# A gather of 128 rows by index, taken from GpSimd and fetched row by row by SyncE and ScalarE

## The chip, the cores and the metric

The kernel runs on one core of a Trainium2 chip. The metric is the device time of one execution in microseconds (us). GpSimd (POOL in the profile), VectorE (DVE), ScalarE (ACT), TensorE (PE) and SyncE (SP) each run their own instruction stream. SP and ACT can also start plain DMAs (rows SPq and ACTq); GpSimd starts the indirect ones, that is those whose rows are picked by a list of indices.

## The reference, cut to what matters

Four graph layers run over 12,500 nodes and 400,000 edges that are sorted by destination. What the change touches is the fetching of source rows in layers 2 and 3:

```python
def _L2_gnn_ref(feat, weight, src, dst, etypes):
    h_src = feat[src]
    for r in range(num_rels):
        mask = etypes == r
        msg = msg + h_src * mask[:, None] @ weight[r]
    return segment_sum(msg, dst, n)

def _L3_gnn_ref(...):
    m = concatenate([x[row], x[col], edge_attr], axis=1)
    h = maximum(m @ W1 + b1, 0.0)
    h = maximum(h @ W2 + b2, 0.0)
    h = h @ W3 + b3
    # segment sum, count and segment max of h over col
```

## The kernel before, in words

Each of the 128 partitions owns 3,125 consecutive edges (T). In the three edge stages one step takes one edge of each partition, so one step needs 128 rows of a table in DRAM, and one `indirect_dma_start` on GpSimd fetches them (`gather`, line 132). A step of the scan then is one or two VectorE instructions that add the fetched rows to a running sum, which starts anew where the destination changes.

**Edge stage 2** (`edges_2`) fetches rows of `Y`, the product of every node with the weights of every relation: 64 floats, 256 bytes. The steps are grouped in slots of 25 (SL2), five slots (NS2) make a chunk of 125 steps, and there are 25 chunks. ScalarE copies the indices of a slot into `idx` (L1484) once VectorE has finished that slot of the chunk before; GpSimd issues 25 gathers of the slot on semaphore `got[q]`; VectorE waits for all 25 and runs 25 steps (L1526); SyncE waits for `run_ready` and stores the slot (L1459) and a block of zeros (L1460). Buffers exist for five slots, so the same slot of the next chunk may be filled once VectorE is through with it, some four slots ahead of its use.

**Edge stage 3** (`edges_3`) fetches rows of `ytab`, 32 floats, 128 bytes. Slots have 16 steps (SL3), a chunk four slots (NS3) or 64 steps; 48 whole chunks and a tail of 53 steps follow each other. Per slot TensorE waits for the gathers and then multiplies by the weights (L1795), adds the spread destination part (L1798) and the gathered part (L1800) through the identity, ScalarE applies the ReLU (L1849), TensorE the second layer (L1807), ScalarE again (L1862), TensorE the third (L1814), and VectorE runs 16 steps of two instructions each (L1920, L1922). SyncE stores the slot (L1749). GpSimd may refill a buffer when `pre` says that TensorE has read it.

**Edge stage 1** (`edges_01`) has, besides its own gathers, a list of chores that VectorE does between its slots. The last of them clears a part of `X` for which SyncE waits before it loads `X` (L793, L794).

Each engine runs its list strictly in order; an instruction that waits on a semaphore holds all that stands behind it on that engine. The loops are hardware loops (`Fori`), with addresses worked out in registers.

Of the kernel before, what the change touches and what calls it, by code (L numbers as in the profile page):

```python
# [21 lines left out]
D = 64  # L22
# [4 lines left out]
MSG = 32  # L27
# [23 lines left out]
SL2 = 25  # L51
# [84 lines left out]
def scatter(eng, table, index, in_, sem, add=False):  # L136
    kw = {"compute_op": ALU.add} if add else {}
    eng.indirect_dma_start(out=table, out_offset=bass.IndirectOffsetOnAxis(ap=index, axis=0),
                           in_=in_, in_offset=None, **kw).then_inc(sem, 16)


# [192 lines left out]
def edges_01(nc, k, ins):  # L334


    with ExitStack() as ctx:
# [3 lines left out]
        def sem(name):  # L341
# [9 lines left out]
        cum5 = sb("cum5", [NB, P])  # L351
        row_f, row_i = sb("row_f", [P, NB]), sb("row_i", [P, NB], I32)
        limit_i, limit, found = sb("limit_i", [P, NB], I32), sb("limit", [P, NB]), sb("found", [P, NB])
        v64, v16 = sb("v64", [P, NQ, SG, D]), sb("v16", [P, NQ, SG, A16])
# [49 lines left out]
            sem(s) for s in ("idx_decoded", "sameS_ready", "same_ready", "pre_scanned"))  # L404
        idx_ready, metas, scanned, x_clear = (sem(s) for s in ("idx_ready", "metas", "scanned", "x_clear"))
        l_some, hot5_ready, summed5, cum5_ready, counted5, limit_ready, rows_ready, fined, ends_found, turned_ends = (
            sem(s) for s in ("l_some", "hot5_ready", "summed5", "cum5_ready", "counted5", "limit_ready", "rows_ready",
# [32 lines left out]
        def _(v):  # L440
# [156 lines left out]
            def chores():  # L597
# [24 lines left out]
                for i, (kind, e, _) in enumerate(sortA.steps):  # L622
# [3 lines left out]
                    else:  # L626
# [22 lines left out]
                                              in1=k.rel_i[:, :], op0=ALU.mult, op1=ALU.add))  # L649
                yield 3.4, None  # L650
                s.done(v.tensor_scalar(found[:, :], found[:, :], 0.5, SC / 2, ALU.mult, ALU.add))
# [3 lines left out]
                yield 3.8, None  # L655
                v.memset(k.X[96:P, LASTN:NB, :], 0.0).then_inc(x_clear, 1)

            work = chores()
# [98 lines left out]
        def _(sp):  # L757
# [58 lines left out]
            sp.wait_ge(settled, 16 * (NW + 5 + 3 + 6))  # L816

# [74 lines left out]
        def _(pe):  # L892
# [48 lines left out]
            for i in range(3):  # L941
# [5 lines left out]
                             start=True, stop=True).then_inc(rows_built, 1)  # L947

            pe.wait_ge(ends_found, 1)
            nc.tensor.transpose(k.ps[0:NB, 0, 0:P], found[:, :], k.ident[:, :]).then_inc(turned_ends, 1)  # L950
# [475 lines left out]
def edges_2(nc, k, ins):  # L1426

    with ExitStack() as ctx:  # L1428
# [10 lines left out]
        got = [sem(f"msg_got{q}") for q in range(NS2)]  # L1439
        stored = [sem(f"stored2_{q}") for q in range(NS2)]  # L1440
        late = [sem(f"msg_late{i}") for i in range(SL2 // PART2)]
        meta_ready, run_ready, part_ready, vsteps, zero_put = (
# [3 lines left out]
        LAST = CHUNKS2 - 1  # L1446
        PARTS = SL2 // PART2

        def last_slot(c, q):
# [5 lines left out]
        def _(sp):  # L1455
            def slot(c, q):
# [31 lines left out]

        @block.gpsimd
        def _(pool):  # L1490
            def slot(c, q):
                hold(pool, meta_ready, 2 * (NS2 * c + q + 1), k.passed)
                for t in range(SL2):
                    gather(pool, msg[:, q, t, :], k.Y, idx[:, q, t:t + 1],
                           late[t // PART2] if last_slot(c, q) else got[q])

            def body(c):
                for q in range(NS2):
                    slot(c, q)

            turns(pool, LAST, body)
            body(LAST)

        @block.vector
        def _(v):
# [3 lines left out]
            def slot(c, q, part):  # L1509
                if not is_first(c):  # L1510
                    v.wait_ge(stored[q], 16 * c)
                for t in range(SL2):
                    if t % part == 0:
                        if last_slot(c, q):
                            v.wait_ge(late[t // part], 16 * part)
# [180 lines left out]
def edges_3(nc, k, ins):  # L1696

    with ExitStack() as ctx:
# [16 lines left out]
        same = sb("same3", [P, NS3, SL3])  # L1715
        anew = sb("anew", [P, NS3, SL3])
        loaded = [sem(f"loaded3{q}") for q in range(NS3)]
        got = [sem(f"y_got{q}") for q in range(NS3)]
# [27 lines left out]
        def _(sp):  # L1746
# [3 lines left out]

            with sp.Fori(0, CHUNKS3) as c:
                for q in range(NS3):
                    store(c, q)
            for q, steps in enumerate(TAILS3):
                store(CHUNKS3, q, steps)
# [4 lines left out]
        def _(pool):  # L1760
            def slot(c, q, steps):
                hold(pool, idx_ready, NS3 * c + q + 1, k.passed)
                if not is_first(c):

                    hold(pool, pre, NS3 * c + q + 1 - NS3, k.passed)
                for t in range(steps):
                    gather(pool, yg[:, q, t * MSG:(t + 1) * MSG], k.ytab, idx[:, q, t:t + 1], got[q])

# [9 lines left out]
        def _(pe):  # L1778
            def slot(c, q, steps):
# [12 lines left out]
                pe.wait_ge(zready, n + 1)  # L1792
                pe.wait_ge(got[q], 16 * SL3 * c + 16 * steps)
                for a, b, w in cuts(steps):
                    nc.tensor.matmul(ps(1, q)[0:w, a:b], k.W1e[0:w, 0:w], eaT[0:w, m, a:b], start=True, stop=False)  # L1795
                    for g, _ in groups(steps):
                        if a <= g < b:
# [353 lines left out]
def build(nc, ins, out):  # L2151
    with ExitStack() as ctx:
# [67 lines left out]
        k.R1, k.R2, k.R3 = dram("R1", [E + P, R1W]), dram("R2", [E + P, D]), dram("R3", [E + P, 2 * MSG])  # L2220
        k.Y = dram("Y", [NP * RELS, D])
        k.ytab, k.ztab, k.Z = dram("ytab", [NP, MSG]), dram("ztab", [NP, MSG]), dram("Z", [E + NP, MSG])

# [31 lines left out]
```

## Time and profile before

| | |
|---|---|
| median of 3 runs | 12908.45 us (12907.69, 12908.45, 12933.81) |
| the profiled execution's own time | 12933.84 us |
| its span, first to last instruction | 12932.1 us |
| POOL busy | 9682.6 us, 75% |
| DVE busy | 6177.7 us, 48% |
| PE busy | 2650.0 us, 20% |
| ACT busy | 1253.2 us, 10% |
| DMA queues, share of 16 engines | 12.8% + 11.7% + 5.8% |

DMA-issuing instructions of SP and ACT are not counted as busy; they are rows of their own, SPq and ACTq. For GpSimd the gather is counted. The shares are means over stages with different limits, so the rows that follow are taken stage by stage.

### The profile page before, as it was taken

The numbers are of one execution on the slowest core, as the hardware profiler recorded it, in microseconds if no ns is written. First come the engines' busy times: TensorE is split into PE (matmuls) and PEld (weight loads), VectorE is DVE, ScalarE is ACT, GpSimd is POOL, SyncE is SP. The second block draws the span as 40 slices with busy tenths as digits, with TensorE's granted clock in tenths as the row PEclk, the third lists the DMA queues.
The fourth block names the chain that finished last, engine by engine and source line by source line (L and its number), as shares of the span: only waits on it lengthen the run. The fifth ranks groups of instructions, "written<-read, shape, count | busy, mean of one in ns | idle before, by whom it ended". The sixth has DMA issues, their size and how long they took to land. (4 is left out here: it accounts for less than half of the span.)

```text
span 12932.1 us, 78820 instructions
## 1 busy us (share of the span) xinstructions
PE 2650.0 (20%) x12045; PEld 1931.0 (15%) x12072; DVE 6177.7 (48%) x21573; ACT 1253.2 (10%) x3613; POOL 9682.6 (75%) x10104
## 2 busy tenths in 40 slices
PE   2000011111100720000000000013444444444445
PEld 2000011111100410000000000012322222333223
DVE  8877377777733532222222222224555555555555
ACT  3111111111111420000000000000010000000001
POOL 7777777777777767777777777777777777777776
PEclk6555555555555865555555555555666666666666
DMA  6444444444443432222222222222222222222221
GB/s 168 119 117 117 120 120 117 117 117 117 115 120 110 145 102 64 64 68 64 64 65 67 64 64 68 64 51 54 65 67 65 65 65 67 65 65 67 65 65 48
DMA packets 732388, 1103.27 MB, mean 85 GB/s; under 512 B 241571, under 2 KB 348032, under 8 KB 731407
## 3 DMA queue, kind: packets, MB, share of 16 engines
q0 software_dynamic: 332944, 306.83, 12.8%
q1 hardware_dynamic: 232318, 567.30, 11.7%
q10 hardware_dynamic: 167040, 228.30, 5.8%
q14 instruction: 70, 0.57, 0.0%
q8 instruction: 16, 0.26, 0.0%
HBM read 548.69 MB, written 552.93 MB: 85 GB/s over the span
## 5 line engine op out<-in xcount | busy, mean ns | idle before, releaser
L132 POOL DMA_INDIRECT msg<-Y,idx x3125 | 2969.1, 950 | 1016.1 <-issue 952.5
L132 POOL DMA_INDIRECT yg<-ytab,idx x3125 | 2956.8, 946 | 963.4 <-issue 949.5
L132 POOL DMA_INDIRECT g<-in_edge_attr,idxs x3072 | 2959.7, 963 | 938.4 <-issue 857.4
L1526 DVE SCALAR_TENSOR_TENSOR run<-run,same,msg 128x64 f32<-128x64 f32 x3125 | 891.3, 285 | 3033.9 <-DMA msg<-Y,idx 2926.5
L1920 DVE SCALAR_TENSOR_TENSOR run<-run,same,ps 128x32 f32<-128x32 f32 x3125 | 774.7, 248 | 1643.3 <-PE ps L1814 1540.3
L586 DVE SCALAR_TENSOR_TENSOR run<-run,sameD 128x80 f32<-128x80 f32 x3072 | 907.5, 295 | 1327.5 <-DMA g<-in_edge_attr,idxs 889.2
L1114 PE MATMUL ps<-tail,before 128*128 128x64 f32 (+2 forms) x10 | 2.8, 421 | 4582.3 <-PEq L1428 3935.0
L1903 DVE SCALAR_TENSOR_TENSOR zx<-zx,same,zs 128x32 f32<-128x32 f32 x3124 | 792.4, 254 | 136.3 <-DVE anew L1886 28.9
L590 DVE SCALAR_TENSOR_TENSOR runS<-runS,sameS,g 128x64 f32<-128x64 f32 x3072 | 850.8, 277 | 0.0
L1795 PE MATMUL ps<-eaT,W1e 128*128 128x512 f32 (+1 forms) x394 | 401.0, 1121 | 1975.8 <-DMA yg<-ytab,idx 1975.2
L1922 DVE SCALAR_TENSOR_TENSOR run<-run,anew,ps 128x32 f32<-128x32 f32 x3125 | 757.9, 243 | 0.0
L958 PE MATMUL ps<-hot 128*98 128x128 bf16 x3072 | 373.0, 314 | 1820.1 <-DVE hot L682 1820.1
L1114 PEld LDWEIGHTS ps<-tail,before 128*128 128x128 f32 x10 | 2.4, 320 | 4582.9 <-issue 4582.9
L958 PEld LDWEIGHTS ps<-hot 128*98 128x98 bf16 x3072 | 332.6, 202 | 1860.6 <-DVE hot L682 1860.6
L1798 PE MATMUL ps<-ident,zx 128*128 128x128 f32 x1564 | 466.6, 399 | 0.0
L1798 PEld LDWEIGHTS ps<-ident,zx 128*128 128x128 f32 x1564 | 430.0, 318 | 201.7 <-issue 201.7
L1800 PE MATMUL ps<-ident,yg 128*128 128x128 f32 x1564 | 446.1, 383 | 0.0
L682 DVE TENSOR_TENSOR hot<-ps,digits 128x2048 bf16<-128x2048 f32 x192 | 437.3, 2278 | 0.0
L1795 PEld LDWEIGHTS ps<-eaT,W1e 128*128 128x128 f32 (+1 forms) x394 | 98.1, 309 | 2033.2 <-issue 1547.4
L1849 ACT ACTIVATE h<-ps 128x512 f32<-128x512 f32 (+1 forms) x197 | 116.9, 594 | 2858.3 <-PE ps L1800 2858.3
L1484 ACT COPY idx<-rel_i 128x25 int32 (+1 forms) x125 | 26.6, 213 | 3738.4 <-DVE run L1526 3735.2
L1800 PEld LDWEIGHTS ps<-ident,yg 128*128 128x128 f32 x1564 | 388.8, 304 | 0.0
(346 smaller groups left out, 5978.5 us busy)
## 6 DMA issues: line engine op xcount, KB each, us to landing
R<-run SPq DMA_DIRECT2D x390, 320.0 KB, 2.4
R<-run SPq DMA_DIRECT2D x195, 512.0 KB, 2.7
R<-run SPq DMA_DIRECT2D x124, 800.0 KB, 3.8
v<-in_edge_attr ACTq DMA_DIRECT2D x384, 256.0 KB
RA<-runS SPq DMA_DIRECT2D x256, 256.0 KB, 3.1
Y<-tab SPq DMA_DIRECT2D x98, 512.0 KB
msg<-Y,idx POOLq DMA_INDIRECT x3125, 2.4
Z<-zeros SPq DMA_DIRECT2D x125, 400.0 KB, 4.2
```

The lines of the kernel that those rows point to most:

```text
L132: eng.indirect_dma_start(out=out, out_offset=None, in_=table, in_offset=bass.IndirectOffsetOnAxis(ap=index, axis=0)).then_inc(sem, 16)
L586: s.done(v.scalar_tensor_tensor(out=run80[:, q, t], in0=p80, scalar=sameD[:, q, t:t + 1], in1=run80[:, q, t], op0=ALU.mult, op1=ALU.add))
L590: last = v.scalar_tensor_tensor(out=runS[:, q, t], in0=pS, scalar=sameS[:, q, t:t + 1], in1=g64[:, q, t], op0=ALU.mult, op1=ALU.add)
L682: v.tensor_tensor(h[:, :, NB:], over(k.ps[:, 6, 0:P], 1, HB), over(digits[:, 1, at], 2, P), ALU.is_equal).then_inc(hot_ready, 1)
L958: last = nc.tensor.matmul(k.ps[0:NB, which, 0:P], hot[:, i % 2, t, 0:NB], hot[:, i % 2, t, NB:], start=isinstance(c, int) and c == a and i ...
L1526: ins_ = v.scalar_tensor_tensor(out=run[:, q, t, :], in0=prev, scalar=same[:, q, t:t + 1], in1=msg[:, q, t, :], op0=ALU.mult, op1=ALU.add)
L1795: nc.tensor.matmul(ps(1, q)[0:w, a:b], k.W1e[0:w, 0:w], eaT[0:w, m, a:b], start=True, stop=False)
L1798: nc.tensor.matmul(ps(1, q)[0:w, g:g + P], zx[:, q, g:g + w], k.ident[:, :], start=False, stop=False)
L1800: last = nc.tensor.matmul(ps(1, q)[0:w, g:g + P], yg[:, q, g:g + w], k.ident[:, :], start=False, stop=g + P >= b)
L1903: last = v.scalar_tensor_tensor(out=o, in0=p, scalar=same[:, q, t:t + 1], in1=zs[:, q, t * MSG:(t + 1) * MSG], op0=ALU.mult, op1=ALU.add)
L1920: s.done(v.scalar_tensor_tensor(out=run[:, q, t, 0:MSG], in0=p[:, 0:MSG], scalar=same[:, q, t:t + 1], in1=h, op0=ALU.mult, op1=ALU.add))
L1922: b = v.scalar_tensor_tensor(out=run[:, q, t, MSG:], in0=p[:, MSG:], scalar=anew[:, q, t:t + 1], in1=h, op0=ALU.add, op1=ALU.max)
```

## The change

In stage 2, of each chunk's 125 steps, step 12 of slots 1 to 4 is no longer gathered by GpSimd. SyncE fetches it for slots 1 and 3 and ScalarE for slots 2 and 4, with one plain DMA for each of the 128 rows. In stage 3, of each chunk's 64 steps, step 8 of slot 1 is fetched so by SyncE. The place of each row is a byte offset in a register; 32 registers are loaded at a time. The offsets are computed by VectorE in stage 1, turned by TensorE so that one step's 128 offsets lie in one row, saved to DRAM by SyncE, and fetched into one partition ahead of each tile. GpSimd leaves out these steps; the waits of VectorE and TensorE are split in two. In TensorE's stage 3 the waits move behind the first matmul of a slot.

```diff
+def row_bytes(ap):
+    return ap.bitcast(U8).rearrange("(o r) b -> o (r b)", o=1)
+
+def fetch_rows(nc, eng, offsets, out, table, size, sem):
+    for a in range(0, P, ROW_REGS):
+        _, rows = nc.values_load_multi_w_load_instructions(
+            offsets[0:1, a:a + ROW_REGS], engines=[eng.engine], min_val=0, max_val=table.shape[1] - size, ...)
+        for i, row in enumerate(rows):
+            eng.dma_start(out[a + i:a + i + 1, :].bitcast(U8), table[:, bass.ds(row, size)]).then_inc(sem, 16)
...
 stage 1, VectorE's chores
+                v.tensor_scalar(rows2[:, 0:CHUNKS2, :], ..., 4.0 * D, None, ALU.mult).then_inc(rows_listed, 1)
+                v.tensor_scalar(rows3[:, 0:CHUNKS3], ..., 4.0 * MSG, None, ALU.mult).then_inc(rows_listed, 1)
...
+                v.wait_ge(rows_turned, 1)
+                v.tensor_copy(rows2T[:, :], ps_rows2).then_inc(rows_int, 1)
+                v.tensor_copy(rows3T[:, :], ps_rows3).then_inc(rows_int, 1)
...
 stage 1, SyncE
+            sp.wait_ge(rows_int, 2)
+            for to, rows in ((k.rows2, rows2T), (k.rows3, rows3T)):
+                sp.dma_start(to, rows[:, :]).then_inc(settled, 16)
...
 stage 1, TensorE
+            pe.wait_ge(rows_listed, 2)
+            nc.tensor.transpose(ps_rows2, ...)
+            nc.tensor.transpose(ps_rows3, rows3[:, :], k.ident[:, :]).then_inc(rows_turned, 1)
...
 edges_2
+        def row_tile(eng, c, q):
+            eng.wait_ge(listed[q], 16)
+            eng.sem_clear(listed[q])
+            fetch_rows(nc, eng, lists[:, q, :], msg[:, q, ROW_AT2, :], Yb, 4 * D, by_row[q])
+            list_rows(eng, c + 1, q)
...
+            for q in SP_ROWS:
+                row_tile(sp, 0, q)
             with sp.Fori(0, LAST) as c:
                 for q in range(NS2):
                     slot(c, q)
+                    if q in SP_ROWS:
+                        row_tile(sp, c + 1, q)
...
                     act.copy(same[:, q], k.same[:, at]).then_inc(meta_ready, 1)
+                    if q in ACT_ROWS:
+                        row_tile(act, c, q)
...
+            for q in ACT_ROWS:
+                list_rows(act, 0, q)
             turns(act, CHUNKS2, body)
...
                 for t in range(SL2):
+                    if t == ROW_AT2 and q in BY_ROW:
+                        continue
                     gather(pool, msg[:, q, t, :], k.Y, ...)
...
-                            v.wait_ge(got[q], 16 * SL2 * (c + 1))
+                            v.wait_ge(got[q], 16 * (SL2 - (q in BY_ROW)) * (c + 1))
+                            if q in BY_ROW:
+                                v.wait_ge(by_row[q], 16 * P * (c + 1))
...
 edges_3
+            list_rows(0)
+            row_tile(0)
+            with sp.Fori(0, LAST) as c:
                 for q in range(NS3):
                     store(c, q)
+                    if q == ROW_SLOT3:
+                        row_tile(c + 1)
...
-                pe.wait_ge(got[q], 16 * SL3 * c + 16 * steps)
                 for a, b, w in cuts(steps):
                     nc.tensor.matmul(ps(1, q)[0:w, a:b], k.W1e[0:w, 0:w], eaT[0:w, m, a:b], start=True, stop=False)
+                    if a == 0:
+                        if by_rows(c, q):
+                            pe.wait_ge(by_row, 16 * P)
+                            pe.sem_clear(by_row)
+                        pe.wait_ge(got[q], ...)
```

## Rows read from the trace of the kernel before

**Rows 1.** The page, part 1: busy us (share) x instructions per engine.
```profile
PE 2650.0 (20%) x12045; PEld 1931.0 (15%) x12072; DVE 6177.7 (48%) x21573; ACT 1253.2 (10%) x3613; POOL 9682.6 (75%) x10104
```
**Rows 2.** Costliest groups: line, engine, op, out<-in, count | busy, mean ns | idle before, releaser.
```profile
L132 POOL DMA_INDIRECT msg<-Y,idx x3125 | 2969.1, 950 | 1016.1 <-issue 952.5 <-ACT same L1485 63.6
...
L132 POOL DMA_INDIRECT yg<-ytab,idx x3125 | 2956.8, 946 | 963.4 <-issue 949.5 <-ACT idx L1829 10.8 <-PE ps L1800 3.0
...
L1526 DVE SCALAR_TENSOR_TENSOR run<-run,same,msg 128x64 f32<-128x64 f32 x3125 | 891.3, 285 | 3033.9 <-DMA msg<-Y,idx 2926.5
```
**Rows 3.** The tiles msg and yg: ns min/median/max, first and last start in us.
```profile
L132 POOL DMA_INDIRECT msg<-Y,idx x3125: 941/947/1007, 4644.3 to 8565.0; - x196
L132 POOL DMA_INDIRECT yg<-ytab,idx x3125: 941/947/977, 8848.6 to 12757.1; - x196
```
**Rows 4.** Waits, whole span: who waited for whom, us in total, times, longest.
```profile
SPq L1749 <- DVE run L1922: 3799.7, 196, 38.1
SPq L1459 <- DVE run L1526: 3755.3, 124, 41.0
...
ACT idx L1484 <- DVE run L1526: 3735.2, 120, 40.0
```
**Rows 5.** Timeline of VectorE and GpSimd late in one slot of stage 2: start, length.
```profile
6025.44 7.98 DVE L1526 SCALAR_TENSOR_TENSOR run<-run,same,msg 128x64 f32<-128x64 f32 x25 [23.44 <-DMA msg<-Y,idx]
...
6026.56 0.95 POOL L132 DMA_INDIRECT msg<-Y,idx  x1 [0.30 <-issue]
6027.82 0.98 POOL L132 DMA_INDIRECT msg<-Y,idx  x1 [0.30 <-issue]
...
6034.23 0.94 POOL L132 DMA_INDIRECT msg<-Y,idx  x1 [0.30 <-issue]
6035.48 0.95 POOL L132 DMA_INDIRECT msg<-Y,idx  x1 [0.31 <-issue]
```
**Rows 6.** Timeline of SyncE's stores in the same stage.
```profile
6002.18 0.33 SPq L1459 DMA_DIRECT2D R<-run  x1
6002.70 0.33 SPq L1460 DMA_DIRECT2D Z<-zeros  x1
6033.61 0.33 SPq L1459 DMA_DIRECT2D R<-run  x1
```
**Rows 7.** Timeline of SyncE at the kernel's start: loads of weights, fixed addresses.
```profile
34.95 0.29 SPq L781 DMA_DIRECT2D b2b<-in_L_gnn_b  x1
35.28 11.54 SPq L781 DMA_DIRECT2D W2r<-in_L_gnn_weight  x2
...
57.12 0.29 SPq L781 DMA_DIRECT2D b<-in_L_gnn_b  x1
57.45 0.31 SPq L781 DMA_DIRECT2D W1e<-in_L_gnn_W  x1
57.81 0.42 SPq L781 DMA_DIRECT2D W2e<-in_L_gnn_W  x1
58.27 0.42 SPq L781 DMA_DIRECT2D W3e<-in_L_gnn_W  x1
```
**Rows 8.** Timeline of SyncE and ScalarE where both issue a DMA at once.
```profile
1598.05 0.26 SPq L794 DMA_DIRECT2D X<-in_x  x1
...
1598.13 0.36 ACTq L1015 DMA_DIRECT2D v<-in_edge_attr  x1
```
**Rows 9.** The page, part 6: DMA issues, KB each, median us to landing.
```profile
msg<-Y,idx POOLq DMA_INDIRECT x3125, 2.4
```
**Rows 10.** Timeline of one slot of stage 3, engine by engine, to the store.
```profile
10010.94 2.04 PE L1795 MATMUL ps<-eaT,W1e 128*128 128x512 f32 x2 [10.90 <-DMA yg<-ytab,idx]
10012.78 0.63 PE L1798 MATMUL ps<-ident,zx 128*128 128x128 f32 x2
...
10016.06 0.60 ACT L1849 ACTIVATE h<-ps 128x512 f32<-128x512 f32 x1 [15.40 <-PE ps L1800]
...
10018.77 1.92 PE L1814 MATMUL ps<-W3e,h 128*128 128x128 f32 x8 [0.87 <-ACT h L1862]
...
10020.73 0.25 DVE L1920 SCALAR_TENSOR_TENSOR run<-run,same,ps 128x32 f32<-128x32 f32 x1 [8.87 <-PE ps L1814]
...
10027.93 0.33 SPq L1749 DMA_DIRECT2D R<-run  x1
```
**Rows 11.** Timeline of stage 1: TensorE after the chores, SyncE at the load of X.
```profile
1347.72 0.45 PE L950 MATMUL ps<-ident,found 128*98 128x128 f32 x1 [35.91 <-DVE found L653]
1621.83 1.94 PE L958 MATMUL ps<-hot 128*98 128x128 bf16 x16 [273.66 <-DVE hot L682]
...
1597.15 0.86 SPq L793 DMA_DIRECT2D X<-in_x  x2
```
**Rows 12.** The page, part 3: DMA queues, packets, MB, share of 16 engines.
```profile
q0 software_dynamic: 332944, 306.83, 12.8%
q1 hardware_dynamic: 232318, 567.30, 11.7%
q10 hardware_dynamic: 167040, 228.30, 5.8%
```

More of the change, by code:

```diff
@@ L7 @@
 I32 = mybir.dt.int32
+U8 = mybir.dt.uint8
 ALU = mybir.AluOpType
@@ L61 @@
 TAILS3 = [min(SL3, TAIL3 - a) for a in range(0, TAIL3, SL3)]
+ROW_AT2, ROW_AT3, ROW_SLOT3 = 12, 8, 1
+ROW_REGS = 32
+SP_ROWS, ACT_ROWS = (1, 3), (2, 4)
+BY_ROW = (1, 2, 3, 4)
 LANES = 2
@@ L139, in scatter @@
                            in_=in_, in_offset=None, **kw).then_inc(sem, 16)
+def row_bytes(ap):
[3 more added lines that the diff above has]
+        _, rows = nc.values_load_multi_w_load_instructions(
+            offsets[0:1, a:a + ROW_REGS], engines=[eng.engine], min_val=0, max_val=table.shape[1] - size,
+            skip_runtime_bounds_check_because="the byte at which a row of the table begins")
+        for i, row in enumerate(rows):
+            eng.dma_start(out[a + i:a + i + 1, :].bitcast(U8), table[:, bass.ds(row, size)]).then_inc(sem, 16)
 def over(ap, axis, n):
@@ L405, in edges_01 @@
         idx_ready, metas, scanned, x_clear = (sem(s) for s in ("idx_ready", "metas", "scanned", "x_clear"))
+        rows_listed, rows_turned, rows_int = (sem(s) for s in ("rows_listed", "rows_turned", "rows_int"))
+        ps_rows2 = k.ps[0:(CHUNKS2 + 1) * len(BY_ROW), 7, 0:P]
+        ps_rows3 = k.ps[0:CHUNKS3 + 1, 7, P:2 * P]
         l_some, hot5_ready, summed5, cum5_ready, counted5, limit_ready, rows_ready, fined, ends_found, turned_ends = (
@@ L649, in chores @@
                                               in1=k.rel_i[:, :], op0=ALU.mult, op1=ALU.add))
-                yield 3.4, None
+                s.done(v.memset(rows2[:, CHUNKS2, :], 0.0))
+                s.done(v.memset(rows3[:, CHUNKS3:], 0.0))
+                s.wait(s.n)
+                v.tensor_scalar(rows2[:, 0:CHUNKS2, :], k.rel_i[:, :].rearrange("p (c q t) -> p c q t", q=NS2, t=SL2)
+                                [:, :, BY_ROW[0]:, ROW_AT2], 4.0 * D, None, ALU.mult).then_inc(rows_listed, 1)
+                v.tensor_scalar(rows3[:, 0:CHUNKS3], k.src_i[:, 0:CHUNKS3 * CH3].rearrange("p (c t) -> p c t", t=CH3)
+                                [:, :, ROW_SLOT3 * SL3 + ROW_AT3], 4.0 * MSG, None, ALU.mult).then_inc(rows_listed, 1)
+                yield 3.8, None
                 s.done(v.tensor_scalar(found[:, :], found[:, :], 0.5, SC / 2, ALU.mult, ALU.add))
@@ L815, in _ @@
                 sp.wait_ge(storedS[q], 16 * C2)
-            sp.wait_ge(settled, 16 * (NW + 5 + 3 + 6))
+            sp.wait_ge(settled, 16 * (NW + 5 + 3 + 2 + 6))
         @block.gpsimd
@@ L1440, in edges_2 @@
         stored = [sem(f"stored2_{q}") for q in range(NS2)]
+        lists = sb("lists2", [1, NS2, P], I32)
+        listed = {q: sem(f"listed2_{q}") for q in BY_ROW}
+        by_row = {q: sem(f"by_row2_{q}") for q in BY_ROW}
         late = [sem(f"msg_late{i}") for i in range(SL2 // PART2)]
@@ L1447, in edges_2, with list_rows @@
         PARTS = SL2 // PART2
+        Yb = row_bytes(k.Y)
+        def list_rows(eng, c, q):
+            eng.dma_start(lists[:, q, :], k.rows2[bass.ds(c * len(BY_ROW) + BY_ROW.index(q), 1), :]).then_inc(listed[q], 16)
+        def row_tile(eng, c, q):
[3 more added lines that the diff above has]
+            list_rows(eng, c + 1, q)
         def last_slot(c, q):
@@ L1460, in slot @@
                 sp.dma_start(Z[:, bass.ds(at * MSG, SL2 * MSG)], k.zeros[:, 0:SL2 * MSG]).then_inc(zero_put, 16)
+            for q in SP_ROWS:
+                list_rows(sp, 0, q)
+            for q in SP_ROWS:
+                row_tile(sp, 0, q)
             with sp.Fori(0, LAST) as c:
@@ L1474, in _ @@
                 sp.wait_ge(stored[q], 16 * (LAST + (PARTS if q == NS2 - 1 else 1)))
+            for q in BY_ROW:
+                sp.wait_ge(listed[q], 16)
             sp.wait_ge(zero_put, 16 * NS2 * CHUNKS2)
@@ L1716, in edges_3, with by_rows @@
         anew = sb("anew", [P, NS3, SL3])
+        lists = sb("lists3", [1, P], I32)
+        listed, by_row = sem("listed3"), sem("by_row3")
+        ytab = row_bytes(k.ytab)
+        def by_rows(c, q):
+            return q == ROW_SLOT3 and not (isinstance(c, int) and c == CHUNKS3)
         loaded = [sem(f"loaded3{q}") for q in range(NS3)]
@@ L1749, in store, with list_rows, row_tile @@
                 sp.dma_start(R3[:, bass.ds(c * CH3 + q * SL3, steps), :], run[:, q, 0:steps]).then_inc(stored[q], 16)
-            with sp.Fori(0, CHUNKS3) as c:
+            def list_rows(c):
+                sp.dma_start(lists[:, :], k.rows3[bass.ds(c, 1), :]).then_inc(listed, 16)
+            def row_tile(c):
+                sp.wait_ge(listed, 16)
+                sp.sem_clear(listed)
+                fetch_rows(nc, sp, lists[:, :], yg[:, ROW_SLOT3, ROW_AT3 * MSG:(ROW_AT3 + 1) * MSG], ytab, 4 * MSG, by_row)
+                list_rows(c + 1)
+            list_rows(0)
+            row_tile(0)
+            with sp.Fori(0, LAST) as c:
                 for q in range(NS3):
                     store(c, q)
+                    if q == ROW_SLOT3:
+                        row_tile(c + 1)
+            for q in range(NS3):
+                store(LAST, q)
+            sp.wait_ge(listed, 16)
             for q, steps in enumerate(TAILS3):
@@ L1766, in slot @@
                 for t in range(steps):
+                    if by_rows(c, q) and t == ROW_AT3:
+                        continue
                     gather(pool, yg[:, q, t * MSG:(t + 1) * MSG], k.ytab, idx[:, q, t:t + 1], got[q])
```

11 lines of the change are left out of this document (10 added, 1 removed).

## The prediction, made before the changed kernel had been run

> **What bounds the kernel now.** First the page's busy times [rows 1]: POOL has 75% of the span, the next engine 48%. Then the groups by line [rows 2]: in each of stages 2 and 3 GpSimd issues 3125 gathers of about 0.95 us, and the idle time ahead of them (952.5 and 949.5 us, some 0.30 us each) is put down to "issue": it waits for no one, it is simply on its way to the next gather. The tiles give the pace [rows 3]: (8565.0 - 4644.3) / 3124 = 1.255 us from gather to gather in stage 2, (12757.1 - 8848.6) / 3124 = 1.251 us in stage 3. Everybody else waits for that: SP 3755 us and 3800 us, ACT 3735 us [rows 4], DVE 2927 us for the gathered rows [rows 2]. So in these two stages, 7829 us together, the time is the number of gathers times 1.25 us, and SP and nearly all of ACT's sequencer are free.
>
> **What is taken away.** Stage 2: 4 gathers in each of 25 chunks, 100 x 1.255 = 125.5 us. Stage 3: one in each of 48 chunks, 48 x 1.251 = 60.0 us. Together 185.5 us, all on the path, as long as the tiles fetched by row arrive in time.
>
> **What a tile by row costs.** Call its issue time T. No row shows a DMA of one row whose address comes from a register. The nearest is a bias: one row of 64 floats, the very size of a row of `Y`, at a fixed address. It takes 0.29 us, and the next DMA starts 0.33 us after it (34.95 to 35.28, 57.12 to 57.45) [rows 7]; loads over more partitions come at 0.46 us. 128 x 0.33 = 42 us is the lower end. The upper end is the pace of two DMAs inside a loop with addresses worked out in registers: 6002.18 to 6002.70, 0.52 us [rows 6], of which 0.19 us is register work; 128 x 0.52 = 67 us. Here the address needs no arithmetic, only that a register be loaded, 32 at a time, and no row shows such a load. I take 0.33 us plus a third of that register work, 0.06 us, for the load and the use of the register: T = 128 x 0.39 = 50 us, range 42 to 67. I lean to the low side because the two bias rows match the transfer in size and shape, and the loop's stores don't.
>
> **Does it fit in stage 2?** A chunk will take 121 x 1.255 = 151.9 us. SP has two tiles and ten other DMAs in it: 2T + 10 x 0.52 = 105 us at T = 50, 139 us at 67. It is the bound from T = 73. ACT has two tiles and ten short copies, the same. What is queued behind a tile: on SP the stores of the slots that end meanwhile, each late by up to T less the 30 us of a slot, some 20 us (37 at most); DVE needs that buffer back four slots, 120 us, later. On ACT the index copy of the next slot, late by as much; GpSimd too needs it some four slots later. The tile of a slot is asked for when DVE is through with that slot of the chunk before, and has 152 us less T, less a landing of 2.4 us [rows 9] and DVE's 8 us [rows 5]: 90 us to spare. At the stage's start ACT issues two lists ahead of the first index copy, which GpSimd waits for: + 0.9 us. The first tiles (50 us) are asked for at once and used at 62 us or later.
>
> **Does it fit in stage 3?** Here the fit is tight and forms a loop: SP starts the tile for chunk c + 1 only behind the store of slot 1 of chunk c; TensorE waits for the tile in slot 1 of c + 1; and the store of that slot starts the next tile. Round trip: T, landing 2.4 us [rows 9], then from the first L1798 at 10012.78 to SP's store at 10027.93, 15.2 us [rows 10] (L1795, 2 us, now runs ahead of the wait), then the store itself, 0.5 us [rows 6]. That is T + 18.1. GpSimd's chunk will be 63 x 1.251 = 78.8 us. So the round trip is hidden up to T = 60.7, and at T = 50 has 10 us to spare. Beyond it each microsecond of T costs 47 us. The stores of slots 2, 3 and 0 wait behind the tile up to 30 us; DVE wants those buffers three slots (59 us) on. At the stage's start the tile comes some 12 us behind slot 1's gathers, made up in two chunks. GpSimd refills slot 1 only when `pre` of the chunk before is there, about 30 us early at this T.
>
> **The rest, costed at nothing.** The lists: two short DVE operations, two memsets and two copies, two transposes. Their TensorE is idle for 35.9 us ahead of L950 and 273 us behind it, and SP comes to the load of X at 1597 us, 250 us after L950 [rows 11]; stage 1 is paced by its gathers and would hand back a delay of 2 us. If that cover were gone it would cost 2 us. The 512 new DMAs of a chunk carry 256 bytes each, and the queues stand at 12.8, 11.7 and 5.8% [rows 12]. What could touch the path is a slower gather: beside DVE's steps it takes 0.98 in place of 0.95 us [rows 5]. If DMA writes did the same to all 6100 gathers it would take back 180 us; but a slot's store, issued at 6033.61 [rows 6], lands beside gathers of 0.94 and 0.95 us [rows 5], so I take none, and a bound of a tenth, 20 us.
>
> **The sum.** 185.5 - 0.9 = 184.6 us. The profiled execution took 12933.84 us (span 12932.1) and would take 12749; it was 25.4 us above the median of the runs, 12908.45, against which I forecast 12908.45 - 184.6 = 12724, rounded to 12725.
>
> **Rivals.**
> (a) The register costs as much as the loop's register work, 0.19 us a row. T = 67: the round trip in stage 3 is 85.1 us against 78.8, 47 x 6.3 = + 296 us, and the kernel comes to about 13020, slower than before. It decides from T = 60.7 on, and passes break-even at 64.6 (47 x 3.9 = 185). For it: every register-addressed DMA in the trace has that gap [rows 6]. Against it: those addresses are computed, these are not. The Trainium skill, "Runtime: NRT & Kernel Launch", on instruction fetch, speaks for this rival: it puts a register load at some 200 ns per register even in bulk. By that page the sum would be T = 42 + 26 = 68 us and a time of about 13065. No row of this case shows such a load.
> (b) The two queues cannot issue at once, so that the four tiles of stage 2 follow each other: 4 x 42 = 168 us + 5 us of stores against 151.9 is + 21 us a chunk, 25 x 21 = + 525, less 185: about 13250. Against it: at 1598 us SP and ACT issue with 0.18 us of overlap and take 0.26 and 0.36 us [rows 8], no more than alone. The Trainium skill, "Perfetto Trace Analysis", section on HWDGE DMA instructions, says that the descriptor generator is shared and locked by the one who uses it, which is this rival. The trace disagrees, but with one short overlap.
> (c) No change: T within 0.6 us of 64.6, where stage 3 gives back what both stages gain (12882 to 12934). For it: the middle of T's range, 54, isn't far; against it, how narrow the window is.
> (d) T above 73, both stages bound by the issue: 13300 and far more. For it only that a register load is unknown.
>
> **How the numbers follow.** Forecast, T up to 60.7: 0.64, its own range 12700 to 12760. T between 60.7 and 64.0, a little faster: 0.06. (a) 0.15, (b) 0.06, (c) 0.05, (d) 0.04. A measurement of this kernel can tell about 0.2% (26 us) from no change. Faster 0.70, within 0.2% 0.05, slower 0.25. The range 12700 to 13060 takes in the forecast, the small gain, (c) and most of (a), some 0.87, and leaves out (b) and (d).
>
> **What would show each step.** 3025 gathers on `msg` and 3077 on `yg` at 1.255 and 1.251 us; stage 2 from its first to last gather 3795 us, stage 3 3849 us. T is read from SPq: first to last of 128 issues, 42 to 60 us. In stage 3 TensorE's wait ahead of L1798 must still be put down to the indirect DMA; if it is the row DMA in slot 1 and GpSimd waits for `pre`, the round trip rules. The issue times of SP and ACT in stage 2 beside SP's alone in stage 3 decide (b). The prediction is wrong if T is over 61 us.

## The result, and the profile after

The changed kernel takes 12723.22 us (median of 4 runs, 12718.36 to 12744.54) against 12908.07 us before: the ratio is 0.9855, with a 95% interval of 0.9838 to 0.9872. The forecast was 12725.

| | before | after |
|---|---|---|
| profiled execution, its own time | 12933.84 us | 12744.54 us |
| span | 12932.1 us | 12742.7 us |
| gathers of stage 2 and of stage 3 | 3125, 3125 | 3025, 3077 |
| stage 2, first to last gather | 3920.7 us | 3796.6 us |
| stage 3, first to last gather | 3908.5 us | 3849.4 us |

The page of the changed kernel, part 1, answers to [rows 1] (busy us, share, instructions), and part 3 to [rows 12]:

```profile
PE 2970.5 (23%) x12074; PEld 2055.6 (16%) x12074; DVE 6179.3 (48%) x21579; ACT 1252.9 (10%) x3613; POOL 9537.5 (75%) x9956
...
q0 software_dynamic: 328208, 302.76, 12.8%
q1 hardware_dynamic: 257781, 569.91, 12.3%
q10 hardware_dynamic: 179944, 229.99, 6.1%
q14 instruction: 597, 4.89, 0.1%
```

GpSimd has 148 gathers fewer and is as busy in share as before: it still sets the pace. The DMA queues of SP and ACT (q1 and q10) rose by less than a point each, though 18,944 row DMAs were added.

The tiles of the changed kernel (ns min/median/max, first and last start in us) answer to [rows 3]:

```profile
L159 ACTq DMA_DIRECT2D msg<-Y x6400: 228/229/1100, 4640.7 to 8350.5; - x194
L159 SPq DMA_DIRECT2D msg<-Y x6400: 227/228/568, 4641.2 to 8320.4; - x194
L137 POOL DMA_INDIRECT msg<-Y,idx x3025: 941/947/997, 4638.6 to 8435.2; - x190
...
L159 SPq DMA_DIRECT2D yg<-ytab x6144: 227/228/400, 8719.7 to 12452.2; - x199
L137 POOL DMA_INDIRECT yg<-ytab,idx x3077: 941/947/977, 8717.0 to 12566.4; - x193
```

(8435.2 - 4638.6) / 3024 = 1.256 us and (12566.4 - 8717.0) / 3076 = 1.251 us from gather to gather, as before: the row DMAs don't slow GpSimd. Stage 2 gave 124.1 us and stage 3 59.1. The span fell by 189.4 us; the other 6 lie outside: stage 2 started 5.7 us earlier, and 1.8 us went between the two stages, while the end took 1.3 more.

SP's timeline in stage 2 (start, length; a merged row spans its instructions) answers to [rows 6]:

```profile
6077.43 0.33 SPq L1516 DMA_DIRECT2D Z<-zeros  x1
6082.10 48.84 SPq L159 DMA_DIRECT2D msg<-Y  x128
6131.15 0.23 SPq L1497 DMA_DIRECT2D lists<-rows  x1
6131.64 0.39 SPq L1515 DMA_DIRECT2D R<-run  x1
6132.22 0.37 SPq L1516 DMA_DIRECT2D Z<-zeros  x1
```

A tile of 128 rows takes 48.8 us (48.7 to 50.1 over the stage), and 4.3 us pass between the end of the store ahead of it and its first row. ScalarE at the same time:

```profile
6018.71 53.58 ACTq L159 DMA_DIRECT2D msg<-Y  x128
...
6075.56 0.21 ACT L1548 COPY idx<-rel_i 128x25 int32 x1 [58.91 <-issue]
```

The index copy at 6075.56 has waited for the tile ahead of it in ScalarE's list, as was foreseen. It costs nothing: apart from the one wait at the start of the stage (61.3 us, 63.6 before [rows 2]), GpSimd's gathers on `msg` wait for "issue" alone.

At the start of stage 2 both queues issue from the first moment on:

```profile
4641.21 49.08 SPq L159 DMA_DIRECT2D msg<-Y  x128
```
```profile
4640.75 50.37 ACTq L159 DMA_DIRECT2D msg<-Y  x128
```

Side by side for all of its 49 us, SP's tile takes what it takes elsewhere.

### The profile page after: what moved, and what is told of

It reads as the page before. It is cut to its first block and busy times, and to the rows that moved or that the text cites. A ratio compares the mean times of both kernels' runs of the same rounds, so it can differ in the third digit from the quotient of the medians.

```text
span 12742.7 us, 117881 instructions
## 1 busy us (share of the span) xinstructions
PE 2970.5 (23%) x12074; PEld 2055.6 (16%) x12074; DVE 6179.3 (48%) x21579; ACT 1252.9 (10%) x3613; POOL 9537.5 (75%) x9956
## 5 line engine op out<-in xcount | busy, mean ns | idle before, releaser
L137 POOL DMA_INDIRECT yg<-ytab,idx x3077 | 2911.6, 946 | 949.4 <-issue 920.1
L137 POOL DMA_INDIRECT msg<-Y,idx x3025 | 2874.0, 950 | 984.8 <-issue 923.5
L1901 PE MATMUL ps<-ident,zx 128*128 128x128 f32 x1564 | 524.8, 439 | 1460.6 <-DMA yg<-ytab,idx 1430.5
L1901 PEld LDWEIGHTS ps<-ident,zx 128*128 128x128 f32 x1564 | 416.9, 326 | 1738.6 <-DMA yg<-ytab,idx 1705.2
L1903 PE MATMUL ps<-ident,yg 128*128 128x128 f32 x1564 | 488.8, 416 | 0.0
L1903 PEld LDWEIGHTS ps<-ident,yg 128*128 128x128 f32 x1564 | 422.4, 329 | 0.1
L1893 PE MATMUL ps<-eaT,W1e 128*128 128x512 f32 (+1 forms) x394 | 369.4, 1036 | 141.9 <-ACT eaT L1946 130.9
L1917 PE MATMUL ps<-W3e,h 128*128 128x128 f32 x1564 | 354.7, 399 | 170.2 <-ACT h L1965 170.2
L1917 PEld LDWEIGHTS ps<-W3e,h 128*128 128x128 f32 x1564 | 306.4, 291 | 416.1 <-issue 412.2
```

The costliest lines, as they stand in the source:

```text
L137: eng.indirect_dma_start(out=out, out_offset=None, in_=table, in_offset=bass.IndirectOffsetOnAxis(ap=index, axis=0)).then_inc(sem, 16)
L1901: nc.tensor.matmul(ps(1, q)[0:w, g:g + P], zx[:, q, g:g + w], k.ident[:, :], start=False, stop=False)
L1903: last = nc.tensor.matmul(ps(1, q)[0:w, g:g + P], yg[:, q, g:g + w], k.ident[:, :], start=False, stop=g + P >= b)
L1917: last = nc.tensor.matmul(ps(3, q)[:, a:a + w], h2[0:w, m, a:a + P], k.W3e[0:w, 0:w], start=True, stop=True)
```

## The experiments

Each time stands beside runs of the kernel before on the same chip: 12908.25 us for `s2_only`, `s3_only`, `s3_more32` and `five_split`; 12907.65 for `s3_more64`, `five_sp3`, `fixed_rows` and `pe_wait_first`; 12919.5 for `s3_more16_b` and `s2_only_b`. `s3_more64`, `five_sp3` and `fixed_rows` ran twice each, the others at least four times.

**Each stage alone.** `s2_only` puts stage 3 back on GpSimd:

```diff
-            return q == ROW_SLOT3 and not (isinstance(c, int) and c == CHUNKS3)
+            return False
...
-            list_rows(0)
-            row_tile(0)
-            with sp.Fori(0, LAST) as c:
+            with sp.Fori(0, CHUNKS3) as c:
...
-                        pe.wait_ge(got[q], 16 * (SL3 - (q == ROW_SLOT3)) * c + 16 * (steps - by_rows(c, q)))
+                        pe.wait_ge(got[q], 16 * SL3 * c + 16 * steps)
```

TensorE's wait for the gathers stays behind its first matmul here.

> The four tiles of stage 2 alone; step 8 of stage 3 goes back to GpSimd (the lists for stage 3 are still built). Theory of the path: each gather taken from GpSimd is worth its pace, 100 x 1.255 us, so about 125 us below the kernel before, some 12783. Rival, that part of the gain comes from elsewhere (the moved wait of TensorE, say): more than 140 or less than 110 us.

`s3_only` has no rows fetched by SP or ScalarE in stage 2:

```diff
-SP_ROWS, ACT_ROWS = (1, 3), (2, 4)
+SP_ROWS, ACT_ROWS, USED = (), (), ()
...  USED in place of BY_ROW wherever stage 2 gathers, waits or makes a semaphore
```

> The tile of stage 3 alone; stage 2 gathers all of its steps on GpSimd again. Theory of the path: 48 x 1.251 = 60 us below the kernel before, some 12848. Rival, that the round trip of SP and TensorE takes part of it: under 45 us.

`s3_only` took 12845.59 us, 62.7 below before (ratio 0.9955, 0.9938 to 0.9971): the expected 60, within the noise. `s2_only` took 12784, 12785, 12842 and 12871 us, a median of 12813.63 and a ratio of 0.9921 (0.9897 to 0.9944), 30 us short of what was expected. Its profile, the execution of 12871, shows the gain in stage 2 in full and the loss ahead of it. The tiles msg and yg of `s2_only`, then of `s3_only`:

```profile
L137 POOL DMA_INDIRECT msg<-Y,idx x3025: 940/944/1003, 4716.5 to 8506.5; - x190
L137 POOL DMA_INDIRECT yg<-ytab,idx x3125: 940/944/975, 8790.2 to 12691.3; - x196
```
```profile
L137 POOL DMA_INDIRECT msg<-Y,idx x3125: 940/944/1004, 4622.9 to 8538.5; - x196
L137 POOL DMA_INDIRECT yg<-ytab,idx x3077: 940/944/974, 8821.3 to 12663.0; - x193
```

These two profiles compare the stages most finely, for a gather takes 944 ns in both: stage 2 is 3790.0 us against 3915.6, 125.6 less, and stage 3 is 3841.7 against 3901.1, 59.4 less. The node stage of `s2_only` from 4190 us (length of the window, busy us of PE, PEld, DVE, ACT and POOL with instructions, granted clock of TensorE, DMA share, GB/s):

```profile
4190.00:4670.00 480.00, 395.47 (x1320) 205.59 (x1320) 218.46 (x410) 185.16 (x271) 289.56 (x290) 0.67 0.39 125
```

The same stage of the changed kernel:

```profile
4190.00:4590.00 400.00, 300.66 (x1299) 160.98 (x1299) 218.18 (x413) 180.86 (x264) 294.76 (x296) 0.83 0.46 150
```

Stage 2 began 78 us later than in the changed kernel: between the edge stages TensorE has much to do, and its granted clock averaged 0.67 of full speed there, against 0.83. To see whether the kernel does this or the stage varies by itself, the same kernel was run again, and, as the chip was disturbed that time (below), a third time:

> The four tiles of stage 2 alone, again, for the same reason. 12784 us in most executions if the surplus of two of the first four belongs to the node stage, where it was seen.

`s2_only_b` took 12793.87 us (12792.53 to 12795.53), a ratio of 0.9903 (0.9887 to 0.9920): 125.6 us below before. Its four executions lie within 3 us of each other, so the surplus of `s2_only` isn't a fixed cost of the kernel; what sets it off, on another chip and in two executions of four, is open. So the two parts are worth 125.6 and 62.7 us, 188 together, and the whole change gave 185; each of these differences is known to some 20 us either way.

**More rows in stage 3.** The forecast called the fit there tight: a round trip of SP, TensorE and SP again against GpSimd's 78.8 us for a chunk. In the changed kernel it can be read off. SP's timeline, and then TensorE's:

```profile
10034.77 0.33 SPq L1830 DMA_DIRECT2D R<-run  x1
...
10038.66 48.61 SPq L159 DMA_DIRECT2D yg<-ytab  x128
```
```profile
10098.32 0.80 PE L1901 MATMUL ps<-ident,zx 128*128 128x128 f32 x2 [6.74 <-DMA yg<-ytab,idx]
```

From store to first row 3.9 us, the rows 48.6, the landing 2.4 [rows 9], and from L1901 to the store 15.3 (15.2 by [rows 10]): 70.2 us. The last row was issued at 10087.3 and TensorE took the tile at 10098.3, which leaves 8.6 us. The landing of 2.4 us is a gather's. Where the loop runs unhindered, in the first two chunks of the stage, it can be read directly:

```profile
8719.72 48.74 SPq L159 DMA_DIRECT2D yg<-ytab  x128
...
8788.48 48.63 SPq L159 DMA_DIRECT2D yg<-ytab  x128
...
8857.71 48.67 SPq L159 DMA_DIRECT2D yg<-ytab  x128
```

From tile to tile it is 68.8 and 69.2 us, so some 10 us are to spare in a chunk. These kernels put further row DMAs ahead of each tile, into a tile that nobody reads:

```diff
+                for a in range(0, MORE, ROW_REGS):
+                    _, rows = nc.values_load_multi_w_load_instructions(lists[0:1, a:a + ROW_REGS], ...)
+                    for i, row in enumerate(rows):
+                        sp.dma_start(waste[a + i:a + i + 1, :].bitcast(U8), ytab[:, bass.ds(row, 4 * MSG)]).then_inc(by_row, 16)
                 fetch_rows(nc, sp, lists[:, :], yg[...], ytab, 4 * MSG, by_row)
...
-                            pe.wait_ge(by_row, 16 * P)
+                            pe.wait_ge(by_row, 16 * (P + MORE))
```

> 16 more rows in front of each tile of stage 3, again, as the first time the kernel before itself took 15523 us in place of 12908 and nothing could be compared. Theory of a threshold, as before: a round trip of 76.7 us against 78.8, no change from 12723. Rival, a cost that grows with the rows: 12806.

> The changed kernel with 32 more row DMAs in front of each tile of stage 3, into a tile that nobody reads. Theory of the round trip: in the changed kernel it is 3.9 us from store to first row, 48.6 for the rows, 2.4 landing and 15.3 to the next store, 70.2 us, with 8.6 us to spare. 32 more rows are 12.2 us, 82.4 against GpSimd's 78.8, + 3.6 us in each of 47 chunks: some 170 us slower than the changed kernel, about 12890, the whole gain gone. Rival, SP is merely busy and its time hidden (76 of 79 us a chunk would be issue): no change from 12723.

> The changed kernel with 64 more row DMAs in front of each tile of stage 3. Theory of the round trip: 70.2 + 24.3 = 94.5 us against 78.8, + 15.7 us in each of 47 chunks, 740 us slower than the changed kernel, about 13460; TensorE's wait ahead of its second matmul in slot 1 is then for SP's rows and GpSimd waits for TensorE. Rival, SP's issue time alone decides (73 us of rows, 4 of gap, 2 of stores: 79 against 78.8): about 12730.

| more rows | time | ratio to before (95%) | stage 3, first to last gather | round trip, worked out | tile to tile, mean |
|---|---|---|---|---|---|
| 0 | 12723.22 | 0.9855 (0.9838 to 0.9872) | 3849.4 us | 70.2 | 78.4 |
| 16 | 12731.39 | 0.9855 (0.9839 to 0.9871) | 3841.5 us | 77.6 | 78.2 |
| 32 | 12888.97 | 0.9984 (0.9975 to 0.9994) | 4004.3 us | 83.2 | 82.7 |
| 64 | 13509.98 | 1.0466 (1.0446 to 1.0487) | 4619.0 us | 95.7 | 95.6 |

The fifth column adds to 70.2 us the time by which the additional rows put the tile off, 7.4, 13.0 and 25.5 us; the last one is measured. (A gather has a median of 947 ns in the profiles of the kernel before and of the changed one, whose own times lie above their medians, and 944 in the other three: hence 3849.4 beside 3841.5.) SP's timeline, with 16 and then with 32 more rows:

```profile
10020.65 5.17 SPq L1845 DMA_DIRECT2D waste<-ytab  x16
10028.09 48.07 SPq L159 DMA_DIRECT2D yg<-ytab  x128
...
10099.32 5.17 SPq L1845 DMA_DIRECT2D waste<-ytab  x16
```
```profile
10021.72 10.72 SPq L1845 DMA_DIRECT2D waste<-ytab  x32
10034.69 48.49 SPq L159 DMA_DIRECT2D yg<-ytab  x128
...
10103.84 10.73 SPq L1845 DMA_DIRECT2D waste<-ytab  x32
```

16 rows put the tile off by 7.4 us and the chunk still takes 10099.32 - 10020.65 = 78.7 us, GpSimd's time. 32 rows put it off by 13.0 us and this chunk takes 82.1 us. The stage grew by 163 us against the one with 16 rows, and the time by 166 against the changed kernel's; the forecast for 32 rows, 12890, was met, and that for 64, 13460, fell 50 us short. So nothing happens up to the threshold. Beyond it a microsecond costs some 50: from 32 to 64 rows the tile is put off by 12.5 us more, and the time grows by 621. The rivals (half the dose costs 83 us; SP is merely busy and 32 rows change nothing; SP's busy time alone decides, 12730 for 64 rows) all fall. TensorE's wait ahead of the second matmul of slot 1 (L1798 before, L1909 here) is now for SP's rows, the sign that the prediction gave for this case, and GpSimd waits too (us in total, times, longest):

```profile
10084.42 0.79 PE L1909 MATMUL ps<-ident,zx 128*128 128x128 f32 x2 [35.23 <-DMA yg<-ytab]
```
```profile
POOL yg L137 <- ACT idx L1940: 188.3, 60, 10.7
```

The rows had all been issued at 10034.69 + 48.49 = 10083.18 us, and TensorE goes on 1.2 us later: that is the landing of a row fetched by SP, where 2.4 had been put.

GpSimd doesn't wait for TensorE's `pre` itself, as the forecast had it, but for ScalarE's index copy for the next chunk, which stands in ScalarE's list behind its own wait for `pre`.

**A fifth tile in stage 2.** Both kernels take step 12 of slot 0 from GpSimd as well. `five_split` has SP fetch its first 64 rows and ScalarE the last 64:

```diff
+        def half_tile(eng, c, h):
+            eng.wait_ge(halves[h], 16)
+            eng.sem_clear(halves[h])
+            for a in range(h * H, (h + 1) * H, ROW_REGS):
+                ...  32 registers, 32 rows into msg[:, 0, ROW_AT2, :]
+            list_half(eng, c + 1, h)
```

> A fifth tile in stage 2, step 12 of slot 0, half of its rows fetched by SP and half by ScalarE. GpSimd issues 120 gathers a chunk, 150.6 us. SP has 2.5 tiles of 53 us and ten other DMAs, 139 us; ScalarE 2.5 tiles of 56 us, 141 us. Theory: both fit, 25 x 1.255 = 31 us more are gained, about 12692. Rival: ScalarE's late index copies (each behind up to 84 us of tiles) hold GpSimd up and the gain is under 10 us or a loss.

12689.80 us (12686.38 to 12692.96), ratio 0.9833 (0.9817 to 0.9850), 33 us below the changed kernel, as expected; its slowest execution, 12692.96, is faster than the changed kernel's fastest, 12718.36. Stage 2 took 3757.5 us, 32.5 less than in `s2_only`. SP's timeline has the half tile at its price, and little room left in a chunk:

```profile
6030.69 48.53 SPq L160 DMA_DIRECT2D msg<-Y  x128
...
6080.47 0.37 SPq L1534 DMA_DIRECT2D Z<-zeros  x1
6086.07 0.34 SPq L1533 DMA_DIRECT2D R<-run  x1
...
6090.73 23.35 SPq L1520 DMA_DIRECT2D msg<-Y  x64
...
6176.87 48.73 SPq L160 DMA_DIRECT2D msg<-Y  x128
```

From slot 3's tile to slot 3's tile of the next chunk SP takes 146.2 us, not the 139 counted, against GpSimd's 150.6.

`five_sp3` gives the fifth tile to SP whole:

```diff
-SP_ROWS, ACT_ROWS = (1, 3), (2, 4)
+SP_ROWS, ACT_ROWS = (0, 1, 3), (2, 4)
-BY_ROW = (1, 2, 3, 4)
+BY_ROW = (0, 1, 2, 3, 4)
...
```

> The fifth tile of stage 2 goes to SP whole: three tiles of 53 us and ten other DMAs are 164 us against GpSimd's 150.6 for 120 gathers. Theory, SP's issue time bounds the stage: 25 x (164 - 151.9) = 300 us slower than the changed kernel, about 13025. Rival, two queues issuing side by side get slower or faster with the load on them: a tile on SP away from 49 us.

13263.30 us, ratio 1.0275 (1.0255 to 1.0296): slower, as expected, but by 540 us in place of 300. The tile keeps its 49 us; a chunk takes 174 us, not 164:

```profile
6009.23 49.32 SPq L160 DMA_DIRECT2D msg<-Y  x128
...
6064.53 49.19 SPq L160 DMA_DIRECT2D msg<-Y  x128
...
6122.17 49.12 SPq L160 DMA_DIRECT2D msg<-Y  x128
...
6172.54 0.37 SPq L1517 DMA_DIRECT2D Z<-zeros  x1
6178.10 0.34 SPq L1516 DMA_DIRECT2D R<-run  x1
...
6183.25 49.05 SPq L160 DMA_DIRECT2D msg<-Y  x128
```
```profile
6176.03 16.02 DVE L1601 SCALAR_TENSOR_TENSOR run<-run,same,msg 128x64 f32<-128x64 f32 x50 [45.10 <-DMA msg<-Y]
```

The three tiles with what stands ahead of their first rows take 161 us, and ten stores and three list loads 8, where 159 and 5 had been counted. The rest is a pause of 5.2 us once a chunk (6172.9 to 6178.1), between the stores of slot 4 and of slot 0 of the next chunk, that is where SP's loop turns. SP doesn't wait for VectorE there: VectorE had been idle for 45 us before 6176.03, waiting for rows fetched one by one, and what it began then lasts to 6192. `five_split` has the same pause at the same place (6080.8 to 6086.1 above). A part that SP's loop itself costs had thus been left out; what happens in it, no run shows. 22 us over GpSimd's 151.9 in 25 chunks are 550 us, which fits the 540.

**What a register costs.** `fixed_rows` fetches the same number of rows from fixed places:

```diff
-        _, rows = nc.values_load_multi_w_load_instructions(
-            offsets[0:1, a:a + ROW_REGS], ...)
-        for i, row in enumerate(rows):
-            eng.dma_start(out[a + i:a + i + 1, :].bitcast(U8), table[:, bass.ds(row, size)]).then_inc(sem, 16)
+        for i in range(ROW_REGS):
+            row = (a + i) * 90 * size
+            eng.dma_start(out[a + i:a + i + 1, :].bitcast(U8), table[:, row:row + size]).then_inc(sem, 16)
```

> All row DMAs read fixed rows of the tables: no register is loaded or used (the fetched values are not those of the edges, the work is the same). Prices the register. In the changed kernel 128 rows take 48.8 us on SP, 0.38 a row. Theory of the forecast: a fixed row costs 0.33 us as the bias loads did, so a tile takes 42 us, and the register 0.05. Rival: the register load is nothing and the gaps are code loading: a tile stays at 48 us. The time stays at 12723 by either, as the tiles are hidden.

12719.76 us (12716.00 and 12723.53), no change, as expected. SP's timeline in stage 2, where ScalarE issues too, and in stage 3, where SP is alone:

```profile
6063.94 0.33 SPq L1514 DMA_DIRECT2D Z<-zeros  x1
6064.38 39.46 SPq L157 DMA_DIRECT2D msg<-Y  x128
...
10017.13 0.33 SPq L1828 DMA_DIRECT2D R<-run  x1
10017.57 38.10 SPq L157 DMA_DIRECT2D yg<-ytab  x128
```

A fixed row costs 0.30 to 0.31 us, less than the 0.33 of the forecast, and the first follows the store at once; the rival, a tile of 48 us all the same, falls. With registers the tile takes 48.6 to 48.8 us and starts 3.6 us or more behind the end of the store: 14 us for 128 registers, 0.11 us each. Of these the load of 32 registers is at most 2.25 us (10032.44 to 10034.69 in `s3_more32` above), 0.07 us each, and each row has a register move of 29 ns besides. The rest, 1.3 us ahead of the first row, I can't place.

**TensorE's wait.** `pe_wait_first` moves the wait for GpSimd's gathers back:

```diff
+                pe.wait_ge(got[q], 16 * (SL3 - (q == ROW_SLOT3)) * c + 16 * (steps - by_rows(c, q)))
                 for a, b, w in cuts(steps):
                     nc.tensor.matmul(ps(1, q)[0:w, a:b], k.W1e[0:w, 0:w], eaT[0:w, m, a:b], start=True, stop=False)
                     if a == 0:
                         if by_rows(c, q):
                             pe.wait_ge(by_row, 16 * P)
                             pe.sem_clear(by_row)
-                        pe.wait_ge(got[q], ...)
```

> The changed kernel with TensorE's wait for GpSimd's gathers back ahead of the first matmul in stage 3; the wait for SP's rows stays behind it. Theory: 2 us of matmul go back behind the last gather of each slot, hidden but for the last slot: no change, 12723 within 10 us. The granted clock of TensorE in stage 3 fell from 0.66 to 0.56 with the change; if it is the moved matmul that does it, it is back at 0.66 here, if it is the splitting of the gathers it stays at 0.56.

A median of 12722.89 us (12720.99 to 12818.09; ratio 0.9880, 0.9842 to 0.9919), equal to the changed kernel's: the moved wait is worth nothing here. One of the four executions took 12818, 97 us more, which wasn't profiled. Stage 3 in windows, TensorE first, of the kernel before, the changed one, this one, and `s2_only`, which has the moved wait and no tile by row in this stage:

```profile
8849.00:12759.00 3910.00, 1612.26 (x6231) 1161.51 (x6232) 2102.39 (x9717) 382.37 (x779) 2956.49 (x3125) 0.66 0.24 65
```
```profile
8717.00:12568.00 3851.00, 1925.35 (x6231) 1283.68 (x6232) 2105.50 (x9723) 382.56 (x779) 2911.62 (x3077) 0.56 0.24 67
```
```profile
8707.00:12549.00 3842.00, 1554.16 (x6229) 1106.36 (x6230) 2103.96 (x9717) 381.27 (x777) 2903.69 (x3077) 0.69 0.24 67
```
```profile
8790.00:12693.00 3903.00, 1942.00 (x6231) 1292.54 (x6232) 2106.06 (x9724) 382.51 (x779) 2949.83 (x3125) 0.55 0.25 66
```

The granted clock went 0.66, 0.56, 0.69, 0.55, and TensorE's busy time for the same matmuls 1612, 1925, 1554, 1942 us. So it is the moved matmul and not the tile by row. But the moved matmul doesn't always do it: `s3_more32` and `s3_more64` have it too, at 0.65 and 0.63. There TensorE waits behind the first matmul 50 and 49 times, about once a chunk, in place of 194 times in the changed kernel.

**A disturbed chip.** `s3_more16` and `s2_only_again`, the first tries of the two repeats above, met a chip on which the kernel before took 15523.44 us.

> The changed kernel with 16 more row DMAs in front of each tile of stage 3, half the dose of the 32 that cost 166 us. From those runs a row is 0.335 us and a load of 32 registers 2.25, so 16 rows are 6.5 us and the round trip 70.2 + 6.5 = 76.7, below GpSimd's 78.8. Theory of a threshold: no change from 12723. Rival, a cost that grows with the rows (half of 166): 12806.

> The four tiles of stage 2 alone, a second time, because the first gave 12784, 12785, 12842 and 12871 us, and the profiled one of 12871 spent its surplus in the node stage ahead of stage 2, with TensorE's clock at 0.67 there against 0.82. If that stage varies by itself, most executions are at 12784; if the kernel does it, they stay spread.

They took 18704.64 us (ratio 1.2082, 1.1982 to 1.2182) and 17463.26 us (1.1163, 1.1056 to 1.1270). They tell nothing of 16 rows, but something of the scheme. In `s3_more16` a gather still took GpSimd 0.94 us, and a tile by row had grown from 48 to 77.5 us:

```profile
15079.37 77.52 SPq L159 DMA_DIRECT2D yg<-ytab  x128
```

Whatever slowed that chip cost the kernel before 20% and these two 47 and 36%, by the undisturbed times of the same kernels. Stages with tiles by row suffered most: stage 3 took 6309 us in `s3_more16` and 4956 in `s2_only_again`, which has no such tile there, against 3842 and 3901 undisturbed, 64 and 27% more. The median row DMA kept its 228 ns, but the longest took 1.4 us in place of 0.4. What it was, no run shows.

## Why the prediction was right

**The bound.** That a gather is worth its pace held: from first to last gather stage 2 fell by 124.1 us in the profile and by 125.6 between `s3_only` and `s2_only`, stage 3 by 59.1 and 59.4, against 125.5 and 60.0 in the sum. The times of the two kernels, 125.6 and 62.7 us below before, agree within their noise of 20 us. By the same noise it is luck that 12725 and 12723.22 lie only 2 us apart. The last start minus the first start of a tile, over the count, was the right row to take it from.

**The tile by row.** T was put at 50 us, in a range from 42 to 67, and is 48.8 on SP. The bias rows were the right neighbours: 0.33 us there, 0.30 with fixed rows, 0.335 with registers and without their load. Load and use of the register, guessed at a third of the loop's register work, 0.06 us a row, are 0.08 inside the tile (48.6 against 38.1 us); a fixed row that is cheaper than put and a register that is dearer nearly cancel, which is luck. Two terms were missing. The loads ahead of the first row stand between store and tile, 3.9 us from store to row in stage 3 where 0.5 had been put, while the landing is 1.2 us and not 2.4: the round trip is T + 20.4 and not T + 18.1, 69 us, and would have been hidden only up to T = 58.4, not 60.7. And ScalarE needs 50.0 to 54.1 us for its tile, in the median 53.3, not SP's 48.8. Neither used up its cover. The sum for SP in stage 2 also left out the two list loads and the turn of its loop, which `five_split` and `five_sp3` show to matter once the queue is full.

**Rival (a)**, a register at 0.19 us a row, would have needed T = 67; with all its parts a register costs 0.11. The Trainium skill, "Runtime: NRT & Kernel Launch", on instruction fetch, puts a register load at some 200 ns per register and speaks of loads from HBM. Here the offsets come from SBUF, and a load of 32 measured 2.25 us, 70 ns per register, so that figure doesn't carry over. The mechanism of the rival was sound, though: `s3_more32` made the tile late by just 13 us, and 166 us of the gain of 185 were gone.

**Rival (b)**, that two queues cannot issue at once, is refuted. SP's tile takes 49.1 us with ScalarE issuing beside it from end to end (4641.21 above) and 48.6 us alone in stage 3. With fixed rows it is 39.4 to 40.7 us in most of stage 2, where some of each tile lies beside ScalarE's, and 38.1 alone; only the stage's first few took up to 51.1. The Trainium skill ("Perfetto Trace Analysis", HWDGE DMA instructions) describes a lock on the descriptor generator, held by one DMA instruction until its descriptors are generated, and gives no length for it. The prediction read it as holding back whole tiles; the trace shows no such thing: 49.1 against 48.6 us is 1%.

**Rivals (c) and (d)** needed T above 64 and 73.

**The covers.** The chores of stage 1 cost nothing that shows: stage 2 began 5.7 us earlier than before, not later, though its start varies by some 20 us among the profiles (4622.9 to 4644.3 us, `s2_only` aside), so that a cost of 2 us can't be excluded. The first tile of stage 3 came late, as expected: TensorE waited up to 18.7 us for SP's rows, twice in the whole stage. It cost nothing: GpSimd's waits on `yg` for ScalarE's index copies are 12.5 us, 10.8 before [rows 2]. ScalarE's lists at the start of stage 2 (0.9 us) are too small to see. The gathers kept their median of 947 ns beside the row DMAs. The one term that nobody had counted, TensorE's clock, fell on an engine that is busy for half of stage 3 even so (1925 of 3851 us).

## What to carry to other kernels

Where one engine's issue rate is the bound and its operations are all alike, moving some to idle queues was worth their pace, even where the queue needs forty times as long for the operation (48.8 against 1.25 us), as long as each queue's sum fits in the period. Look for the round trip besides the sum: a queue that must first store before it may fetch for the same buffer has a latency, which is free up to the period and costs its whole excess in every round beyond it. Count what the queue's own loop costs as well: SP's three tiles overran the chunk by 22 us where 12 had been counted. When it fits, measure the slack, and spend it in pieces smaller than the unit (half a tile more to each queue gave 33 us, a whole one more to SP lost 540).

## What the runs showed of the hardware that was not expected

- Starting TensorE's first matmul of a slot ahead of the wait lowered its granted clock in stage 3 from 0.66 to 0.56 of full speed, that is from a mix of its two levels, 1.2 and 2.4 GHz, to one nearer the lower. The same matmuls took 1925 us in place of 1612. With the wait moved back, the rows in two parts staying as they were, it was 0.69 and 1554 us; with the wait moved and the rows in one part (`s2_only`) it was 0.55. The work of a slot was cut in two with a pause between; where the pause came once a chunk and not in every slot (`s3_more32`) it was 0.65. What the gate looks at, these runs don't show.
- A DMA of one row of 128 or 256 bytes at an address from a register takes SP 0.23 us (median), and the next one starts 0.335 us after it; at a fixed address it takes 0.25 us and the next starts after 0.30. A load of 32 registers from SBUF takes SP 2.25 us.
- The rows that SP fetched in stage 3 had landed 1.2 us after the last issue had ended (`s3_more32`; the same in `s3_more64`, 10116.67 to 10117.89 us), half of the 2.4 us of a gather [rows 9].
- ScalarE issues the same rows more slowly than SP: some 53.3 against 49.0 us with registers, 42.5 against 39.8 with fixed rows. Why is open.
- The instruction queue (q14) moved 597 packets in place of 70 in the kernel before, 363 with the tiles of stage 2 alone, 75 with those of stage 3 alone and 81 with fixed rows. That the longer loops of SP and ScalarE have their code loaded anew would explain it, and the pause of 5.2 us where SP's loop turns; neither is shown. In the changed kernel nothing on the path waited for it.
